# B-scaled identities as the moving operand of the token-to-channel products of a selective scan (language-model layer, one Trainium2 core)

## The reference, cut to what matters

```python
proj = u @ x_proj_w                      # u: 8 x 256 tokens x 384 channels
dt = softplus(proj[..., :12] @ dt_w + dt_b)
Bm, Cm = proj[..., 12:28], proj[..., 28:44]          # 16 states each
def step(h, xs):                         # one token after another
    d_t, u_t, B_t, C_t = xs
    h = exp(d_t[..., None] * A) * h + (d_t * u_t)[..., None] * B_t[:, None, :]
    return h, einsum('bdn,bn->bd', h, C_t)
# y_forward + y_backward, layer norm, gate with silu(z), @ W_out,
# then the router, two of eight experts for each token, and the sum
```

## Time and profile before

| | |
|---|---|
| median of 3 runs | 1047.11 us (1046.46 to 1047.38) |
| the profiled execution: its time / its span | 1040.84 / 1039.1 us |
| busy PE / PEld | 764.9 / 665.1 us |
| busy DVE / ACT / POOL | 737.8 / 708.7 / 649.2 us |
| first scan starts, last transposes of the scan stage end | 186.36, 668.34 us |

### The profile page before, as it was taken

The page is one execution under the profiler, slowest core; times in us unless marked ns, Lnnn a source line. Parts: engine busy times, 40 slices in busy tenths (PEclk is TensorE's granted clock), DMA queues, the critical chain, the costliest instruction groups (busy, mean ns, idle before and its releaser), DMA issues. The chain is left out here.

```text
span 1039.1 us, 14980 instructions
## 1 busy us (share of the span) xinstructions
PE 764.9 (74%) x5308; PEld 665.1 (64%) x5309; DVE 737.8 (71%) x836; ACT 708.7 (68%) x1189; POOL 649.2 (62%) x359
## 2 busy tenths in 40 slices
PE   0559772787878778789887888656626887999991
PEld 0225321677777777678776877556525877999991
DVE  4898387899999999999999999964155111222224
ACT  0134895999999999899998999324242444565652
POOL 7435555699998999799998999602113656221120
PEclk9969665899999999999999999986655899899996
DMA  4012101112123112212111222299986752000005
GB/s 85 0 61 121 66 26 28 55 61 82 62 81 123 61 65 79 82 62 76 68 62 70 73 82 81 78 314 211 258 188 149 144 129 60 24 19 23 19 23 190
DMA packets 31902, 91.92 MB, mean 88 GB/s; under 512 B 7560, under 2 KB 15264, under 8 KB 30824
## 3 DMA queue, kind: packets, MB, share of 16 engines
q1 hardware_dynamic: 20792, 57.53, 16.4%
q0 software_dynamic: 8352, 27.07, 12.1%
q10 hardware_dynamic: 2704, 6.61, 1.9%
HBM read 77.67 MB, written 13.53 MB: 88 GB/s over the span
## 5 line engine op out<-in xcount | busy, mean ns | idle before, releaser
L1376 PE MATMUL ps<-ident,arena 128*128 128x128 f32 (+1 forms) x3390 | 433.3, 282 | 171.6 <-DVE arena L818 54.7
L1376 PEld LDWEIGHTS ps<-ident,arena 128*128 128x128 f32 (+1 forms) x3390 | 381.0, 144 | 218.4 <-DVE arena L818 70.2
L559 POOL TENSOR_TENSOR arena<-arena 128x1024 f32<-128x1024 f32 x192 | 426.7, 2248 | 44.0 <-DVE arena L818 41.6
L818 DVE TENSOR_TENSOR_SCAN arena<-arena,ps 128x1024 f32<-128x1024 f32 x192 | 428.0, 2271 | 5.0 <-PE ps L1376 3.6
L1206 ACT ACTIVATE arena<-arena,neg_a 128x510 f32<-128x510 f32 x384 | 241.4, 714 | 0.0
L1192 ACT ACTIVATE arena<-arena 128x384 f32<-128x384 f32 x224 | 116.8, 607 | 9.0 <-PE ps L1376 8.9
L1192 ACT ACTIVATE arena<-ln_in,arena 128x384 f32<-128x384 f32 x224 | 116.8, 609 | 5.5 <-PE ps L1376 5.4
L1035 DVE TENSOR_SCALAR ln_in<-ps 128x768 f32<-128x768 f32 x39 | 37.3, 957 | 112.4 <-PE ps L1619 82.0
L618 POOL DMA_INDIRECT y_rows<-arena x39 | 37.9, 971 | 115.1 <-DVE arena L1040 107.6
L1629 PE MATMUL ps<-arena,ln_in 128*128 x468 | 85.4, 332 | 9.8 <-issue 7.2
L1629 PEld LDWEIGHTS ps<-arena,ln_in 128*128 128x128 f32 x468 | 76.9, 194 | 10.5 <-issue 10.4
(11 more groups left out here) (206 smaller groups left out, 830.0 us busy)
## 6 DMA issues: line engine op xcount, KB each, us to landing
arena<-b_rows SPq DMA_DIRECT2D x64, 512.0 KB, 3.5
arena<-ws SPq DMA_DIRECT2D x16, 576.0 KB, 9.3
arena<-wf POOLq DMA_DIRECT2D x16, 576.0 KB
arena<-hf POOLq DMA_DIRECT2D x16, 576.0 KB
gates_dram<-arena SPq DMA_DIRECT2D x4, 1536.0 KB, 5.1
arena<-gates_dram ACTq DMA_DIRECT2D x3, 1536.0 KB, 12.9
arena<-y_rows SPq DMA_DIRECT2D x4, 768.0 KB, 7.2
arena<-gates_dram SPq DMA_DIRECT2D x1, 1536.0 KB, 8.8
```

The lines of the kernel that those rows point to most:

```text
L559: g_.tensor_tensor(state[i % STATES], state[i % STATES], c_bc[u % C_BUFS], ALU.mult).then_inc(s_mul, 1)
L818: v.tensor_tensor_scan(o, a, x, 0.0, ALU.mult, ALU.add).then_inc(s_scan, 1)
L1376: return mm(o, src, ident[at:at + parts, at:at + parts], start=start, stop=True, is_transpose=True, skip_group_check=True)
```

## The change

ScalarE no longer scales the token rows. For each unit it scales the 128x128 identity by the same B scalars, eight ops of 128x128, into `b_diag`. TensorE multiplies the unscaled rows `dtu_t` (stationary) by these diagonals (moving) into the same banks: out[channel, token] = sum over k of dtu\_t[k, channel] \* diag(B)[k, token]. VectorE's share of the scaling goes. The transposes of `x_transposes_of` become true fp32 matmuls, as many as before. `dtu` and the first C buffer stay at their address.

```diff
-        xt_flat = [cut([PAIR * TG * DI + DB * (ODD - P)]) for _ in range(2)]
+        b_diag = [cut([PAIR, TG, P]) for _ in range(2)]
...
-            def scale_rest(u):
-                dve.wait_ge(s_dtu_t, 8 * g + TG * (d + 1))
-                if u >= 2:
-                    dve.wait_ge(s_x_ps, DB * (u - 1))
-                v.tensor_scalar(xt(u % 2, PAIR - 1, TG - 1), dtu_t[g % 2][d][:, TG - 1, :].rearrange("p (b c) -> p b c", b=DB),
-                                bt[:, TG * g + TG - 1, n:n + 1], None, ALU.mult).then_inc(s_xt_v, 1)
...
-            dve.wait_ge(s_dtu_t, 2 * TG)
-            dve.wait_ge(s_bt, NG)
-            scale_rest(0)
-            scale_rest(1)
...
-                        if blk == DB - 1 and UG * g + r + 2 < NU:
-                            scale_rest(UG * g + r + 2)
...
-            def scale_x(u):
+            def b_diagonals(u):
-                act.wait_ge(s_dtu_t, 8 * g + TG * (d + 1))
                 if u >= 2:
                     act.wait_ge(s_x_ps, DB * (u - 1))
-                for k in range(PAIR * TG - 1):
-                    n, t = divmod(k, TG)
+                for n in range(PAIR):
                     col = NS * d + PAIR * pair + n
-                    last = a.activation(xt(u % 2, n, t), dtu_t[g % 2][d][:, t, :].rearrange("p (b c) -> p b c", b=DB), ACT.Copy, scale=bt[:, TG * g + t, col:col + 1])
-                last.then_inc(s_xt_a, 1)
+                    for t in range(TG):
+                        last = a.activation(b_diag[u % 2][:, n, t, :], ident[:], ACT.Copy, scale=bt[:, TG * g + t, col:col + 1])
+                last.then_inc(s_b_diag, 1)
...
-            def x_transposes_of(i):
+            def x_products_of(i):
                 if blk == 0:
-                    pe.wait_ge(s_xt_a, u + 1)
-                    pe.wait_ge(s_xt_v, u + 1)
+                    pe.wait_ge(s_b_diag, u + 1)
+                    pe.wait_ge(s_dtu_t, 8 * g + TG * (d + 1))
                 if i >= 2:
                     pe.wait_ge(s_scan, i - 1)
                 for n in range(PAIR):
                     for t in range(TG):
-                        last = transpose(ps[:, X_BANK + PAIR * (i % 2) + n, P * t:P * t + P], xt(u % 2, n, t, blk), P)
+                        last = mm(ps[:, X_BANK + PAIR * (i % 2) + n, P * t:P * t + P], dtu_t[g % 2][d][:, t, P * blk:P * blk + P],
+                                  b_diag[u % 2][:, n, t, :], start=True, stop=True)
                 last.then_inc(s_x_ps, 1)
```

More of the change, by code:

```diff
@@ L50 @@
 GATE_W = 2 * TG * DI
+DTU_AT = 37824
 class Steps:
@@ L167, in build @@
         state = [cut([PAIR, GT]) for _ in range(STATES)]
-        ODD = P + 1
-        xt_flat = [cut([PAIR * TG * DI + DB * (ODD - P)]) for _ in range(2)]
+        b_diag = [cut([PAIR, TG, P]) for _ in range(2)]
         dtu_t = [[ln_flat[:, TG * DI * d:TG * DI * (d + 1)].rearrange("p (t c) -> p t c", t=TG) for d in range(2)],
                  [cut([TG, DI]) for _ in range(2)]]
[L172 to L177, removed]
+        used[0] = max(used[0], DTU_AT)
         dtu = cut([DB, GT])
@@ L344, in build @@
         s_ln_y = sem("y_norm_variance_ready")
-        s_xt_a = sem("x_t_scaled_by_scalar")
-        s_xt_v = sem("x_t_scaled_by_vector")
+        s_b_diag = sem("b_diagonals_ready")
         s_x_ps = sem("x_in_banks")
@@ L827, in moments_y @@
                 moments(lambda t: y_all[g][:, t, :], TG * g, TG, mv, s_ln_y)
-            def scale_rest(u):
-                g, pair, d = unit_of(u)
-                n = NS * d + PAIR * pair + PAIR - 1
-                dve.wait_ge(s_dtu_t, 8 * g + TG * (d + 1))
-                if u >= 2:
-                    dve.wait_ge(s_x_ps, DB * (u - 1))
-                v.tensor_scalar(xt(u % 2, PAIR - 1, TG - 1), dtu_t[g % 2][d][:, TG - 1, :].rearrange("p (b c) -> p b c", b=DB),
-                                bt[:, TG * g + TG - 1, n:n + 1], None, ALU.mult).then_inc(s_xt_v, 1)
             def keep_dtu_t(g, d, t):
@@ L1222, in _ @@
             act.wait_ge(s_bt, NG)
-            scale_x(0)
+            b_diagonals(0)
             keep_first_dtu_t(1)
@@ L1229, in _ @@
                 if u + 1 < NU:
-                    scale_x(u + 1)
+                    b_diagonals(u + 1)
                 if u == UG * (NG - 1) + 4:
@@ L1460, in _ @@
                     dtu_transposes(0, d, t, DT_BANK * GT + DB * GT * d + DI * t)
-            def x_transposes_of(i):
+            def x_products_of(i):
                 u, blk = divmod(i, DB)
+                g, _, d = unit_of(u)
                 if blk == 0:
-                    pe.wait_ge(s_xt_a, u + 1)
-                    pe.wait_ge(s_xt_v, u + 1)
+                    pe.wait_ge(s_b_diag, u + 1)
+                    pe.wait_ge(s_dtu_t, 8 * g + TG * (d + 1))
                 if i >= 2:
@@ L1507, in _ @@
                 if i < ITEMS:
-                    x_transposes_of(i)
+                    x_products_of(i)
                 if i >= LAG:
```

## The result

The changed kernel takes 1104.59 us, the median of 4 runs (1102.22 to 1105.61), against 1046.78 us for the kernel before in the same session (1043.98 to 1047.38). The ratio is 1.0555, 95% interval 1.0529 to 1.0580: slower, as forecast, by 57.8 us where I had said 64.3. The forecast was 1111 us in a range of 1098 to 1136, so it was 6.4 us too high.

The account below looks back on a forecast made before the run. TensorE was to replace VectorE as the scan stage's bound: start 184.45, records 532.2, filling 1.3, boundaries 9.9, then the tail to 732.6 us. The stage's 64.3 us growth on the 1047.11 median gave 1111 us, range 1098 to 1136.

Parts of the forecast that it names:

- TensorE becomes the bound: Scan stage: TensorE needs 8.06 us a unit, above VectorE's 6.47 and ScalarE's 6.2; stage grows by 64.3 us.
- skip term's rows: Same-form fp32 matmuls in the scan stage: two records each, 0.112 us a record, so 0.224 us a product.
- rival of four passes: Products in the scan stage cost four transposes, 0.448 us each, adding 344 us: 1455 us; chance 0.02.
- 0.1 us for each satisfied wait: TensorE's 384 waits before product phases and adds cost 0.1 us each though satisfied: 38 us more, 1149; chance 0.10.
- Start: TensorE's scan-stage work begins after ScalarE's last row copy and a hand-over, at 184.45 us.
- Records: TensorE's products, skip, row transposes and adds up to the last but three: 4752 x 0.112 = 532.2 us.
- Filling: At the stage start, products 2 and 3 wait for scans 0 and 1: 1.3 us of TensorE waiting.
- group boundary: TensorE waits for the bank copy and two scans: 3.3 us at each of three boundaries, 9.9 us together.
- The clock: TensorE's clock in the scan stage might fall in three stretches, up to 9 us; none counted, as pauses get shorter.
- ScalarE: Eight 128-column ops a unit at about 0.303 us each, 6.2 us a unit, hidden behind TensorE.
- The first rival: An item's products cost no more than transposes; VectorE stays the bound without L837, 37.8 us faster: 1009 us; chance 0.06.
- break-even: Price of a scan-stage product at which the stage would end at 668.34 us again: 0.182 us.

Follow-up runs that it names:

- one-record kernel: Changed kernel with all eight products of an item replaced by one-record transposes of the unscaled rows, B left out, waits kept: 1043.01 us.
- second trace of before: The kernel before, unchanged, run and traced again: 1047.60 us, scan stage ending at 669.64 us.
- half of C: 512 of 1024 columns of GpSimd's C product left out: changed kernel 1103.85 us, kernel before 1038.93, one-record kernel 1006.89.
- mixed kernels: Changed kernel with four of eight tiles a unit by products, four by scaled rows and transposes: 1046.62 us; with dt*u also moved to VectorE 1042.32.
- five of eight: Changed kernel with five of an item's eight products kept, three made transposes without B: 1047.77 us, ratio 1.0017.
- bf16 kernel: Changed kernel with token rows and B diagonals in bf16: 1039.74 us; with dt*u also moved from GpSimd to VectorE 1044.21.

## Why the prediction was right, and where it was wrong

**TensorE becomes the bound: right, shown.** The skip term's rows gave the price of the new product, and L1450 has it: two records each, 0.111 us apart, 24 records in 2.66 us. The one-record kernel, which differs in those records alone (and so leaves B out), takes the whole loss back. The rival of four passes is out, and so is the one of 0.1 us for each satisfied wait: PE passes them without idle time.

**The sum, term by term.** Start 184.45 forecast, 184.49 measured. So close a hit is in part luck: the same code, traced in the kernels made from the changed one, began its products between 184.68 and 185.15 us and once at 187.57. Records: I took 0.112 us; from the first product to the last (184.49 to about 722.0) 537.5 us less 8.9 of waiting hold 4744 records, 0.1114 each, so 3 us less. Filling: 1.3 forecast, 0.69 + 0.22 = 0.9 measured. A group boundary shows these waits on PE:

```profile
326.42 1.06 PE L1352 MATMUL ps<-ident,arena 128*128 128x128 f32 x8 [0.15 <-DVE arena L817]
...
328.52 2.05 PE L1450 MATMUL ps<-arena 128*128 128x128 f32 x16 [1.04 <-DVE arena L812]
...
332.94 2.05 PE L1450 MATMUL ps<-arena 128*128 128x128 f32 x16 [1.49 <-DVE arena L812]
```

That is 2.7 us where I had 0.2 + 1.3 + 1.8 = 3.3; three make 8.0 in place of 9.9. Together 5 us less, and the stage grew by 59.8 (58.5 against the second trace of before) and not 64.3. The median grew by 57.8; the 2 us between lie within what the later stages vary by. The clock did not fall in these shorter pauses, as I had counted: it was granted at 1.00 from 184 to 200 us and from 318 to 336. At the start that was luck too. In the changed kernel with half of C it was 0.50 until 188 us, and the first 32 records took 5.67 us in place of 3.81.

**ScalarE: right.** Eight 128-column ops start 187.66 and the next work at 189.99: 0.29 us each, against 0.303 extrapolated. It had 138 us to spare.

**The first rival's time, and one sentence behind it: wrong.** I wrote that without L837 and with a cheap product "VectorE would stay the bound", 1009 us. The step that failed is GpSimd's: I took 2.25 us a product, the mean of the earlier trace rows, and compared it only with TensorE's 2.69. Even that mean makes 3 x 2.25 = 6.7 us a unit, more than the 6.47 that I left to VectorE, so the rival's 1009 us could not hold; the one-record kernel took 1043.01. The mean also hides two kinds. The timeline of GpSimd in the kernel before, units 0 and 1:

```profile
193.09 2.00 POOL L559 TENSOR_TENSOR arena<-arena 128x1024 f32<-128x1024 f32 x1 [0.18 <-DVE arena L818]
196.46 2.38 POOL L559 TENSOR_TENSOR arena<-arena 128x1024 f32<-128x1024 f32 x1 [1.37 <-DVE arena L818]
```

Read one by one, every product of units 0, 3, 6, ... takes 2.00 us in that kernel and all others 2.38; those are the units that use the first of three C buffers. In the changed kernel and all made from it with whole products the 2.00 us kind is gone; the shortest product takes 2.34. The line's durations, before and after:

```profile
L559 POOL TENSOR_TENSOR arena<-arena x192: 1987/2370/2411, 188.8 to 665.2; 128x1024 f32<-128x1024 f32 x192
```

```profile
L553 POOL TENSOR_TENSOR arena<-arena x192: 2341/2370/2417, 189.1 to 724.6; 128x1024 f32<-128x1024 f32 x192
```

Here a statement made ahead of the prediction has to be corrected: the first C buffer and `dtu` do **not** stay at their address. Adding up the cuts of the arena, the C buffer was at word 41990 and is at 39360: no multiple of 16 words before, one now, as the other two C buffers and the states are. So the change has a second effect that the code doesn't name: 66 of GpSimd's products became 0.37 us longer, 24 to 25 us of work. TensorE hides it in the changed kernel. In the one-record kernel it falls on the bound, and with 2.34 us from one product to the next GpSimd asks for 7.0 us a unit, as much as VectorE did before. That the address makes the difference is an inference. For it speaks that the two kinds stand in one and the same kernel, and that the mixed kernels, with the first buffer at word 39936, have the slow kind alone. But no run here moved only the buffer, and none put it back at such an address in the mixed kernel, where GpSimd was busy all the time and this might have paid.

The sentence that VectorE sets the pace of the kernel before stays open in part: ScalarE was as full, and no run takes the two apart.

**The break-even** of 0.182 us a product held (five of eight, where the mean price is 0.181), though for that price two engines are level there, and only one was in its sum.

## What to carry to other kernels

Price a true fp32 matmul by a row of the same form before putting it where a transpose was; here it was two records for one on an engine with 18% to spare, and a change that relieved two other engines lost 5.5%. Before counting on an engine's relief, put the next engine's spacing beside it, from its slow kind and not from its mean: with 7.0 us a unit GpSimd left VectorE's relief 0.06 us of room below the 7.06 of before. A work balanced over three nearly level engines gave back little here (0.4%), and a buffer that moves with the arena is part of the diff.

## What the runs showed of the hardware that I had not expected

GpSimd's fp32 product of two operands in place took 2.00 us with its second operand at word 41990 and 2.38 at an address like the first operand's (halved: 1.09 and 1.28 us for 512 columns), beside a scan and without one alike: the last products of the stage, beside no scan, were 1.99 before and 2.34 after. The cause, the address, is the inference named above. The same product beside VectorE's two-input product took up to 3.90, and VectorE's up to 4.79 (bf16 kernel) in place of 1.75. And TensorE's clock over windows of 100 us was 0.95 to 0.98 in the one-record kernel, where the engine pauses, against 1.00 in the changed kernel, where it is the bound.
